# Two-layer graph attention on one core: ScalarE's order in stage 2, the norm of stage 5 before stage 3, and the last stage's sums in five banks

## The reference, cut to what matters

```python
def layer0(h, adj, W, a):                       # h: 8 x 1024 x 128, adj: 8 x 1024 x 1024 of 0 and 1
    Wh = h @ W
    e = (Wh @ a[:128])[:, :, None] + (Wh @ a[128:])[:, None, :]
    e = where(e > 0, e, 0.2 * e)
    att = softmax(where(adj > 0, e, -9e15), axis=2)
    return elu(att @ Wh)
def layer1(x, adj, W, a):                       # the same without elu; W transposed, mask -1e9
    ...
h = maximum(layernorm(x), 0);  x = x + layer0(h, adj, W0, a0)
h = maximum(layernorm(x), 0);  x = x + layer1(h, adj, W1, a1)
```

## Time and profile before

| | us |
|---|---|
| runs of the kernel | 305.19, 306.36, 306.57 |
| median | 306.36 |
| profiled execution, its own time | 305.33 |
| its span in the trace | 303.5 |
| granted TensorE clock over it, share of full speed | 0.999 |
| TensorE matmuls busy | 290.9 (96%) |
| VectorE busy | 268.9 (89%) |
| ScalarE busy | 167.0 (55%) |
| GpSimd busy | 49.5 (16%) |
| transfers: share of the 16 DMA engines' time | 44.0% on SyncE's queue |

### The profile page before, as it was taken

One profiled execution on the slowest core, in us unless ns is written; L12 is line 12 of the kernel. 1 busy time (PEld: TensorE's weight loads), 2 busy tenths in 40 slices (PEclk: granted clock), 3 DMA queues, 4 the chain that ended last, 5 costly groups with the idle time before them and its releaser, 6 DMA issues.

```text
span 303.5 us, 6589 instructions
## 1 busy us (share of the span) xinstructions
PE 290.9 (96%) x2562; PEld 287.9 (95%) x2562; DVE 268.9 (89%) x612; ACT 167.0 (55%) x489; POOL 49.5 (16%) x53
## 2 busy tenths in 40 slices
PE   7999999979889999999999999999999999999795
PEld 7889999979879999999999999999999999999795
DVE  4797899787999989999899989999899989969765
ACT  3378474576384648384593737565393827364300
POOL 2721003300422030303003030201203000400000
PEclk9999999999999999999999999999999999999999
DMA  7999935023590446904585344903575300201011
GB/s 245 416 406 409 406 111 193 2 65 96 182 352 3 142 138 175 377 7 150 198 272 214 141 118 150 357 6 138 163 261 204 109 33 1 71 0 71 0 71 69
DMA packets 15071, 49.50 MB, mean 163 GB/s; under 512 B 2008, under 2 KB 3136, under 8 KB 15040
## 3 DMA queue, kind: packets, MB, share of 16 engines
q1 hardware_dynamic: 14464, 48.69, 44.0%
q10 hardware_dynamic: 576, 0.39, 0.4%
HBM read 44.83 MB, written 4.25 MB: 162 GB/s over the span
## 4 chain that ended last, share of the span: by engine, by line
PE 84%; DVE 5%; ACT 4%; POOL 3%; DMA 2%; issue 1%; ACTq 0%; DVEq 0%; POOLq 0%
PE acc L932 63%; PE prj L877 8%; PE tp L816 5%; ACT xn L376 3%; PE acc L946 2%; POOL rstd L281 2%; PE acc L808 2%; DVE pbuf L655 2%; DMA row_r<-r_rows 1%; PE prj L880 1%; DVE stats L550 1%; POOL shift L284 1%; PE prj L849 1%; PE tp L899 1%; ACT accs L426 1%
## 5 line engine op out<-in xcount | busy, mean ns | idle before, releaser
L932 PE MATMUL acc<-wh,pbuf 128*128 128x129 f32 x1976 | 230.6, 275 | 2.0 <-DVE pbuf L655 1.3
L932 PEld LDWEIGHTS acc<-wh,pbuf 128*128 128x128 f32 x1976 | 226.0, 192 | 3.0 <-DVE pbuf L655 1.2
L655 DVE SCALAR_TENSOR_TENSOR pbuf<-row_r,sqr,adj_sb 128x1024 f32<-128x1024 f32 x127 | 157.5, 1278 | 3.2 <-DMA row_r<-r_rows 2.2
L281 POOL TENSOR_TENSOR rstd<-vareps,neg_half 128x8 f32<-128x8 f32 x15 | 38.5, 2567 | 205.4 <-DVE vareps L568 205.3
L426 ACT ACTIVATE accs<-accs,rec 128x128 f32<-128x128 f32 x120 | 36.7, 389 | 47.7 <-DVE rec L674 47.7
L376 ACT ACTIVATE xn<-x_sb,shift,rstd 128x128 f32<-128x128 f32 x120 | 47.6, 478 | 0.0
L396 ACT ACTIVATE wh<-prj,wh 128x128 f32<-128x128 f32 x120 | 31.8, 356 | 0.0
L877 PE MATMUL prj<-w_ext,hT 128*128 128x130 f32 x240 | 29.3, 275 | 0.0
L877 PEld LDWEIGHTS prj<-w_ext,hT 128*128 128x128 f32 x240 | 28.0, 191 | 0.0
L382 ACT ACTIVATE hT<-tp 128x1024 f32<-128x1024 f32 x15 | 15.3, 1023 | 21.8 <-PE tp L816 21.8
L664 DVE TENSOR_TENSOR accs<-acc,uniform 128x387 f32<-128x387 f32 (+1 forms) x45 | 20.6, 508 | 3.5 <-PE acc L932 3.4
(11 more groups left out here) (105 smaller groups left out, 154.4 us busy)
## 6 DMA issues: line engine op xcount, KB each, us to landing
adj_sb<-in_adj SPq DMA_DIRECT2D x64, 512.0 KB, 6.4
row_r<-r_rows SPq DMA_DIRECT2D x13, 512.0 KB, 4.0
x_sb<-in_x SPq DMA_DIRECT2D x7, 512.0 KB, 6.1
out_x<-x_sb SPq DMA_DIRECT2D x7, 512.0 KB, 3.0
out_x<-x_sb SPq DMA_DIRECT2D x2, 192.0 KB, 1.9
x_sb<-in_x ACTq DMA_DIRECT2D x1, 256.0 KB, 3.6
x_sb<-in_x SPq DMA_DIRECT2D x1, 256.0 KB, 3.4
r_rows<-rT SPq DMA_DIRECT2D x13, 4.0 KB
```

The source lines that it names most:

```text
L281: nc.gpsimd.tensor_tensor(rstd[:, :], vareps[:, :], neg_half[:, :], ALU.pow).then_inc(rstd_ready, 1)
L655: nc.vector.scalar_tensor_tensor(pbuf[:, t, :], row_r[:, n % 2, :], sqr[:, n % 2, 0, t:t + 1], adj_at(b, t), ALU.max, ALU.min).then_inc(p_ ...
L932: mm = nc.tensor.matmul(sum_of(n, i), pbuf[:, t, i * P:(i + 1) * P], wh[:, n % 2, t, :], start=(t == 0 and s == 0), stop=(t == T - 1), ski ...
```

## The change

It has four parts.

1. *ScalarE in stage 2.* Its pass is now written by itself: first the divisions of stage 1, then the hT copy of stage 3, ELU, then the norm of stage 4, and only then the exponentials, `rT` copy and weights of stage 3.
2. *VectorE.* The statistics of stage 5 stand at the start of the pass for stage 3, ahead of its first mask, instead of behind `exp_args(4)`.
3. *Last stage's banks.* The target tiles are summed in five banks: 0 to 2, 3 and 4, and 5 in the three banks of `acc`, 6 and 7 each in a bank of `prj`. There are five parts instead of four, and two seeded tiles.
4. *The seeds* stand ahead of the divisions of stage 14 on ScalarE.

```diff
-    last_parts = [(0, NB), (NB, 2 * NB), (2 * NB, T - 1), (T - 1, T)]
+    last_parts = [(0, 3), (3, 5), (5, 6), (6, 7), (7, 8)]
...
-                nc.scalar.activation(LAST_TILE, uniform[:, LAST % 2, :],
-                                     ACT.Copy).then_inc(seeded_last, 1)
+                for k in range(len(last_parts) - NB):
+                    nc.scalar.activation(prj[:, k, 0:C], uniform[:, LAST % 2, :],
+                                         ACT.Copy).then_inc(seeded_last, 1)
...
                 elu = stages[n - 1][0] == 0
+                if n == AHEAD - 1:
+
+                    scale_accs(n - 1)
+                    copy_hT(n + 1)
+                    elu_exp(n - 1)
+                    normalise(n + 2)
+                    exps(n + 1)
+                    copy_r(n + 1)
+                    scale_wh(n + 1)
+                    copy_hT(n + 2)
+                    continue
                 if n + 1 in LATE:
                     copy_hT(n + 1)
+                if n == LAST:
+                    seed_last()
                 scale_accs(n - 1)
...
-            seed_last()
...
-                        sums, den = LAST_TILE[:, 0:D].unsqueeze(1), LAST_TILE[:, D:C]
+                        sums = prj[:, k - NB, 0:D].unsqueeze(1)
+                        den = prj[:, k - NB, D:C]
...
-                if n + 2 <= LAST and not {n, n + 1, n + 2} & set(LATE):
+                if n + 2 <= LAST and not {n + 1, n + 2} & set(LATE):
                     statistics(n + 2)
                     moments(n + 2)
...
                     exp_args(n + 1)
-                    if n in LATE:
-                        statistics(n + 2)
-                        moments(n + 2)
                     masks(n, (3, 4, 5))
...
-            def sum_of(n, i):
-                k, s = bank_of[i]
-                return LAST_TILE if n == LAST and i == T - 1 else acc[:, k, s * C:(s + 1) * C]
+            def place(n, i):
+
+                if n < LAST:
+                    return bank_of[i]
+                return next((k, i - lo) for k, (lo, hi) in enumerate(last_parts) if lo <= i < hi)
+
+            def sum_at(k, s):
+                bank = acc[:, k, :] if k < NB else prj[:, k - NB, :]
+                return bank[:, s * C:(s + 1) * C]
...
-                    for i, (k, s) in enumerate(bank_of):
+                    for i in range(T):
+                        k, s = place(n, i)
...
-                        if t == 0 and s == 0 and n > 0:
+                        if t == 0 and s == 0 and n > 0 and k < NB:
                             pe.wait_ge(acc_copied, NB * (n - 1) + k + 1)
-                        if t == 0 and n == LAST and i == T - 1:
-                            pe.wait_ge(seeded_last, 1)
+                        if t == 0 and k >= NB:
+                            pe.wait_ge(seeded_last, k - NB + 1)
```

More of the change, by code:

```diff
@@ L108, in gat_two_layers @@
         WA = (prj[:, 0, 0:2], acc[:, 1, 0:2])
-        LAST_TILE = prj[:, 0, 0:C]
         USUM = prj[:, NB - 1, tiles_in[-1] * E:tiles_in[-1] * E + D]
@@ L472, in _ @@
                 elu = stages[n - 1][0] == 0
+                if n == AHEAD - 1:
[8 more added lines that the diff above has]
+                    continue
                 if n + 1 in LATE:
                     copy_hT(n + 1)
+                if n == LAST:
+                    seed_last()
                 scale_accs(n - 1)
-                if n + 1 in LATE or n + 2 in LATE:
-                    elu_exp(n - 1) if elu else None
+                if n + 2 in LATE:
+                    elu_exp(n - 1)
                 if n < LAST:
@@ L483, in _ @@
                         copy_r(n + 1)
-                    if n + 1 not in LATE and n + 2 not in LATE:
+                    if n + 2 not in LATE:
                         elu_exp(n - 1) if elu else None
@@ L696, in last @@
                     dve.wait_ge(acc_done, NB * LAST + k + 1)
+                    w = hi - lo
                     if k < NB:
-                        w = hi - lo
                         nc.vector.tensor_tensor(
@@ L924, in attend @@
                         pe.wait_ge(p_ready, T * n + t + 1)
-                    for i, (k, s) in enumerate(bank_of):
+                    for i in range(T):
+                        k, s = place(n, i)
                         if halved and i == T // 2:
                             pe.wait_ge(p_ready, 1)
-                        if t == 0 and s == 0 and n > 0:
+                        if t == 0 and s == 0 and n > 0 and k < NB:
                             pe.wait_ge(acc_copied, NB * (n - 1) + k + 1)
-                        if t == 0 and n == LAST and i == T - 1:
-                            pe.wait_ge(seeded_last, 1)
-                        mm = nc.tensor.matmul(sum_of(n, i), pbuf[:, t, i * P:(i + 1) * P],
-                                              wh[:, n % 2, t, :], start=(t == 0 and s == 0),
+                        if t == 0 and k >= NB:
+                            pe.wait_ge(seeded_last, k - NB + 1)
+                        mm = nc.tensor.matmul(sum_at(k, s), pbuf[:, t, i * P:(i + 1) * P],
+                                              wh[:, n % 2, t, :],
+                                              start=(t == 0 and s == 0 and k < NB),
                                               stop=(t == T - 1), skip_group_check=True)
@@ L945, in attend_last @@
                         for i in range(lo, hi):
-                            mm = nc.tensor.matmul(sum_of(LAST, i), pbuf[:, t, i * P:(i + 1) * P],
+                            mm = nc.tensor.matmul(sum_at(k, i - lo), pbuf[:, t, i * P:(i + 1) * P],
                                                   wh[:, LAST % 2, t, :], start=False,
```

## The result

| | before | after |
|---|---|---|
| executions timed, us | 305.19, 305.33, 306.36, 306.57 | 298.58, 298.69, 298.74, 298.75 |
| median | 305.85 | 298.72 |
| profiled execution, its own time | 305.33 | 298.75 |
| its span | 303.5 | 296.9 |
| TensorE busy | 290.9 (96%) | 290.6 (98%) |

The recorded ratio is 0.9748, 95% interval 0.971 to 0.9787; the medians lie 7.1 us apart, and their quotient is 0.9767. The profiled execution fell by 6.58 us, against 5.98 forecast.

What follows compares the result with a forecast made beforehand. TensorE was taken to bound the kernel, so only its stops and the work after its last matmul counted. Gains of 3.43, 1.95 and 0.60 sum to 5.98 us: 306.36 - 5.98 = 300.4 us, range 298.8 to 303.2.

Steps and rivals of the forecast that it cites:

- What bounds it, and the three stops in stages 2 and 3: TensorE bounds the kernel; removing its stops in stages 2 and 3 gains 3.43 us.
- the new waits: Stages 2 and 3: TensorE loses 0.21 us at the turn of `r`, 0.69 at `emax`, 0.55 at stage 4's exponentials.
- Is it kept: Stages 4 to 12: VectorE, busy 148.56 of 156 us, still follows TensorE, so the 3.43 us gained stays.
- The last stage: Stage 15: seeds written early end TensorE's wait of 2.05 us; the last mask costs some 0.1; gain 1.95 us.
- The tail: After the last matmuls: splitting them 12, 8, 4, 4, 4 lets VectorE finish earlier; gain 0.60 us.
- A port between two engines: GpSimd's `shift` beside VectorE's masks: stage 5's would be slow again, with 4 us to spare; stage 4's is at risk.
- the sum: Whole kernel: 5.98 us gained, taken from 306.36, the profiled execution's 305.33 plus 1.03 for the median of the runs.
- stage 4's shift caught: Stage 2: `shift` late behind VectorE's masks, norm blocks exponentials; one mask 301.6 us (chance 0.09), worst 307.2 (slower side 0.04).
- decides from 6.5 us on: Lateness of stage 4's `shift` from which its rival decides; it costs over 0.5% from 8 us.
- VectorE can't follow: Rival, stages 4 to 13: VectorE, 95% busy, loses all of the 3.43 us; 303.8 us, chance 0.12.
- the seed's wait is exchanged: Rival, stage 15: the seed's wait is only replaced by one for a bank copy or mask; 302.3 us, chance 0.05.
- The change does nothing: Rival, stages 2 and 3: waits for `xn` came from `shift` itself, not ScalarE's order; 306 us, chance 0.04.

Runs made afterwards that it cites:

- e3: The kernel before with ScalarE's new order in stage 2 and the earlier statistics, last stage unchanged: short executions 301.23 to 301.62 us, 3.9 less; ratio 0.9868.
- e1: The kernel before with only ScalarE's new order in stage 2: short executions 304.03 to 304.57 us, 1.2 less; ratio 0.9949.
- e2: The kernel before with only stage 5's statistics moved ahead of stage 3's first mask: short executions 302.08 to 302.40 us, 2.9 less; ratio 0.9922.
- e4: The kernel before with only five banks and the seeds ahead of the divisions: 302.70 to 302.89 us, 2.6 less; ratio 0.9888.
- e5: The kernel before with only its one seed moved ahead of stage 14's divisions: eight of ten executions 302.88 to 303.63 us; ratio 0.9941.
- e7: The changed kernel with one more GpSimd power ahead of stage 4's: 299.42, 299.80, 299.97 and 301.95 us; ratio 0.9814.
- e11: The changed kernel with two moves on VectorE, in stage 3 and at the end: 298.28, 298.71, 300.41 and 301.70 us; ratio 0.9807.
- e12: The changed kernel with two more GpSimd powers ahead of stage 4's: span 302.6 us, ratio 0.9956.
- e14: The kernel before with stage 2's row spread by TensorE instead of DMA: six executions 305.37 to 305.75 us, four 307.04 to 307.16; ratio 0.9993.
- e9: The changed kernel with both seeds back behind stage 14's divisions: shortest executions 301.16 and 301.38 us; ratio 0.99.

## Why the prediction was right on the stops and wrong in its number

- *What bounds it, and the three stops in stages 2 and 3*: right. Gain in the profiled execution up to the projection of stage 15: 4.01 us, of which 0.15 is there before stage 2's sums, so 3.86; forecast 3.43. The terms that were mis-sized are the new waits: the gaps are 1.10 against 1.45, and counted from start to start of TensorE's matmuls the three cost 1.04, so that 0.41 of the missing 0.43 is there. I had taken 0.1 us and more for each handing-over and the trace shows less. (The forecast's own account, 4.8 less 1.45, gives 3.35 and not the 3.43 that its times give.) e3 and e1, e2 show that it is the pair which gives it, the statistics most.
- *Is it kept*: right. TensorE has no stop from 76.62 to the end of the trace but for a weight load of stage 15 that is 0.15 late.
- *The last stage*: right, 1.98 us against 1.95: the first part of stage 15's second half starts 6.14 earlier where the projection was 4.01 earlier, and 0.15 of that is lost to the last mask, named as the next cover. e4 (with the tail, 2.6) and e5 (the one seed, 1.8) show it without the other parts.
- *The tail*: right, 0.60 against 0.60. VectorE ends at 294.87, 0.6 behind TensorE's last matmul.
- *A port between two engines*: stage 5's `shift` was slow beside the mask (1.15 us), at no cost; stage 4's took 0.20.
- *The step that failed* is in the sum: "the median of the runs is 1.03 above that execution, so 306.36 - 5.98 = 300.4". That carried the 1.03 us over as if it belonged to every execution of any version. It was a mixture: some executions had the profiled one's length and others were 1.5 to 2 us longer, by a granted clock that halves for a while behind the stop in stage 15, or by a late row in stage 2. Which of the two lay in the first runs of before isn't recorded. The change removed the stop and with it, by the counts, most of that part of the mixture (40 of 113 executions against 4 of 45): the changed kernel's executions lie at 298.31 to 298.94, none of them 1 us above the profiled ones. From the profiled execution alone the sum says 299.35. That is 0.60 above the 298.75 measured: 0.43 by the sizes above, 0.15 that the execution was early before stage 2's sums, where the change has not yet begun, and some 0.02 in the last stage. So of the 1.7 us between forecast and median 1.03 are this step.
- *What is luck in it*: the median of three or four executions of a mixture. In the later batches that of before was 305.23, 305.29, 306.52 and 306.90, and 1.03 was a draw from it. The late row is nothing that the change touches (e7 and e11 have it in their traces), so that none fell among the changed kernel's eight executions isn't its merit either, as far as the runs show.
- The reason for the failure: I priced a stop by its own length and looked at the clock of one execution, in which it had not fallen. That a stop of 2 us can cost nearly as much again behind it was not among the rivals at all; it is the one that came out, in the direction of the gain.
- *Rival: stage 4's shift caught*: didn't happen. e7 and e12 fit its mechanism and its price, save that in e12 the clock comes on top. With `shift` 3.9 us late e12's span is still 0.9 below that of before, so "decides from 6.5 us on" would be near 5 (an estimate from these two).
- *Rival: VectorE can't follow* and *the seed's wait is exchanged*: refuted by the trace after. *The change does nothing*: refuted.

## What to carry to other kernels

A stop of the engine that bounds the kernel may cost more than its length. Compare several executions, and ask of a median that lies above the profiled one what the longer executions have, and whether the change touches that, before adding the difference to the forecast. When a step is moved ahead of another in an in-order list, ask what it now waits for: the norm ahead of the exponentials is worth 1.2 us alone (e1), and makes the kernel sensitive to a `shift` that it used to hide.

## What the runs showed of the hardware

- Behind a stop of TensorE of 2.0 to 2.4 us the granted clock was at 0.50 (1.2 GHz) for about 3.5 us in a part of the executions, 1.7 us each (traced in e3, e5, e7 and e14), and stayed at 1.00 in others (the stop of 2.19 in e11, that of 2.27 in e9). With one of 4.06 us all eight executions had a lower mean clock, and the traced one lost 2.5 us behind it. Behind stops of 1.64 us or less no trace shows a fall, and the stop of 2.00 before stage 4's transposes was followed by the full clock wherever it was traced.
- From the issue of the 4 KB write of `r_rows` to the issue of the read that waits for it there were 1.2 us in most traced executions and 2.4 to 2.9 in others at the same place. Why is open, and nothing was tried on it. Other loads beside it are not the reason in e11: the DMA engines have a share of 0.09 from 43 to 44 (0.08 in the changed kernel, where the row is in time), and of 0.01 and 0.00 from 44 to 46.
- A power over 128x8 on GpSimd takes 2.61 us alone, and 1.6 right behind another.
